# Setting up a Metaformer block: weights transposed four blocks to a bank, rows of ones written by DMA, temperatures loaded first

## What is computed

```
def attention(x, temperature, qkv_w, qkv_b, proj_w, proj_b):      # x after a layernorm over the channels
    qkv = x_flat @ qkv_w.T + qkv_b                  # per image 1024 tokens x 576
    q, k = l2norm(q), l2norm(k)                     # 8 heads of 24
    attn = softmax(einsum('bhnd,bhmd->bhnm', q, k) * temperature)
    return einsum('bhnm,bhmd->bhnd', attn, v) @ proj_w.T + proj_b

x = x + attention(ln(x), ...)
t = tokens(x)
# gate: softmax over 4 experts, the best 2 of each token, weights renormalised
h = gelu(einsum('bsd,edh->ebsh', ln(t), w1) + b1)
t = t + sum_e masked[e] * (einsum('ebsh,ehd->ebsd', h, w2) + b2)
```

## Time and profile before

| | |
|---|---|
| median of 3 runs | 2733.79 us |
| the runs | 2739.15, 2733.28, 2733.79 us |
| the profiled execution's own time | 2741.01 us |
| its span, first to last instruction | 2739.1 us |
| mean granted clock of TensorE | 0.971 |
| PE, DVE, ACT, POOL busy | 90%, 61%, 65%, 52% of the span |
| of it the setup | up to 38.66 us, where the next block's first transpose starts |

### The profile page before, as it was taken

The page is one execution under the profiler, slowest core; times in us unless marked ns, Lnnn a source line. Parts: engine busy times, 40 slices in busy tenths (PEclk is TensorE's granted clock), DMA queues, the critical chain, the costliest instruction groups (busy, mean ns, idle before and its releaser), DMA issues. The chain is left out here.

```text
span 2739.1 us, 58873 instructions
## 1 busy us (share of the span) xinstructions
PE 2465.8 (90%) x18693; PEld 1295.9 (47%) x18693; DVE 1683.5 (61%) x4886; ACT 1780.7 (65%) x2228; POOL 1420.5 (52%) x1137
## 2 busy tenths in 40 slices
PE   3699999999989999989999973999999999999975
PEld 2333333333333333333333321777777777777754
DVE  6557766866766766676676655555555555555522
ACT  2487777777778777767777852555565556555542
POOL 2334435534543543543454323677777777777750
PEclk9799999999999999999999987999999999999987
DMA  4221112112112111211211243444444444444429
GB/s 91 58 51 41 50 49 58 48 42 54 51 44 60 48 49 47 58 41 45 59 48 45 77 162 128 179 155 155 177 155 162 169 155 170 160 158 174 153 79 332
DMA packets 160322, 276.49 MB, mean 101 GB/s; under 512 B 21568, under 2 KB 129584, under 8 KB 150624
## 3 DMA queue, kind: packets, MB, share of 16 engines
q1 hardware_dynamic: 141648, 245.37, 27.8%
q0 software_dynamic: 13392, 27.97, 2.8%
q10 hardware_dynamic: 5056, 0.42, 0.3%
HBM read 174.07 MB, written 49.69 MB: 82 GB/s over the span
## 5 line engine op out<-in xcount | busy, mean ns | idle before, releaser
L788 ACT ACTIVATE probs<-ps_s 128x1024 f32<-128x1024 f32 x1024 | 1011.9, 1023 | 282.6 <-PE ps_s L687 260.0
L1360 POOL TENSOR_TENSOR h_split<-h_f,h_split 128x512 f16<-128x512 f32 x444 | 550.7, 1241 | 238.3 <-ACT h_f L1337 231.0
L1333 ACT ACTIVATE h_split<-ps_h,packs 128x512 f16<-128x512 f32 x444 | 305.2, 687 | 391.1 <-PE ps_h L1287 368.8
L1287 PE MATMUL ps_h<-m_xn_t,packs 128*128 128x512 f16 x2220 | 552.4, 380 | 0.5 <-DVE m_xn_t L1422 0.5
L700 PE MATMUL ps_o<-probs,v_aug 128*32 128x512 f32 x4096 | 550.6, 610 | 0.4 <-ACT probs L788 0.4
L1054 POOL TENSOR_TENSOR inv_norm<-sumsq,minus_half 128x16 f32<-128x16 f32 x128 | 378.0, 2953 | 312.4 <-DVE sumsq L997 307.6
L1301 PE MATMUL ps_y<-packs,h_split 128*128 128x192 f16 x5328 | 511.9, 245 | 0.9 <-POOL h_split L1360 0.9
L1301 PEld LDWEIGHTS ps_y<-packs,h_split 128*128 128x128 f16 x5328 | 453.0, 97 | 105.7 <-POOL h_split L1360 1.9
L687 PE MATMUL ps_s<-stacks_odd 98*128 98x512 f16 x1024 | 301.5, 386 | 17.0 <-DMA stacks_odd<-heads 10.2
L687 PE MATMUL ps_s<-even 98*128 98x512 f16 x1024 | 299.0, 383 | 11.6 <-ACT probs L788 5.7
L1337 ACT ACTIVATE h_f<-ps_h,packs 128x512 f32<-128x512 f32 x444 | 302.0, 680 | 0.0
(11 more groups left out here) (213 smaller groups left out, 2812.6 us busy)
## 6 DMA issues: line engine op xcount, KB each, us to landing
packs<-expert_pack SPq DMA_DIRECT2D x74, 1635.0 KB, 6.6
even<-heads SPq DMA_DIRECT2D x192, 96.0 KB, 2.4
stacks_odd<-heads SPq DMA_DIRECT2D x192, 96.0 KB, 2.4
tile_rows<-sorted_rows SPq DMA_DIRECT2D x37, 400.0 KB
tokens<-in_x_dram SPq DMA_DIRECT2D x17, 768.0 KB, 5.3
y_in<-y_tokens SPq DMA_DIRECT2D x16, 768.0 KB, 8.9
out_dram<-y_out SPq DMA_DIRECT2D x16, 768.0 KB, 7.1
even<-heads SPq DMA_DIRECT2D x128, 48.0 KB
```

The costliest lines, as they stand in the source:

```text
L788: act.activation(probs[:, u % PRING, :], ps_s[:, u % 2, :, :].rearrange("p f n -> p (f n)"), ACT.Exp).then_inc(s_probs, 1)
L1287: mm = pe.matmul(ps_h[:, n % HBUF, :], w1(par, slot, w, k), xn_t[0:rows_k, par, c, :], start=(i == 0), stop=(i == 4))
L1333: act.activation(h_split[:, n % HSPLIT, 0, :], ps_h[:, n % HBUF, :], ACT.Gelu, bias=bias1(par, slot, k), scale=1.0 / WSCALE)
L1360: pool.tensor_tensor(h_split[:, n % HSPLIT, 1, :], h_f32[:, n % HBUF, :], h_split[:, n % HSPLIT, 0, :], ALU.subtract).then_inc(s_h, 1)
```

## The change

Three edits, all in the setup.

- The temperatures are loaded by SP's first DMA instead of its eighth, on a semaphore of their own (`s_temps`). DVE waits for that one before the shift, and for the two biases at the end of the block.
- DVE's two memsets of the rows of ones are gone. SP issues two DMAs instead that copy a tile of ones (`ones16`, made by POOL) into both stacks, 2 partitions x 64 x 128 half precision values each, after its loads and before the stores into `sorted_rows`.
- PE transposes four blocks of 96 into one bank before it signals, so that there are six groups in place of 24 single blocks; DVE copies a group out with one instruction of 384 columns, or with two of 192 where a group spans the gap between the two weights.

```
@@ sync
+            sp.dma_start(temps[:, :], temp.rearrange("h a b -> (a b) h").to_broadcast([P, NH])).then_inc(s_temps, 16)
             for lo in (0, C):
                 sp.dma_start(w_src[:, 0:6, lo:lo + C], wv).then_inc(s_wload, 16)
                 sp.dma_start(w_src[:, 6:WJ, lo:lo + C], wp).then_inc(s_wload, 16)
...
-            sp.dma_start(temps[:, :], temp.rearrange("h a b -> (a b) h").to_broadcast([P, NH])).then_inc(s_bload, 16)
+
+            sp.wait_ge(s_const, 6)
+            for stack in stacks:
+                sp.dma_start(stack[KROWS:SROWS, 0, :, :].rearrange("r h n -> r (h n)").rearrange("r (a b) -> r a b", b=P),
+                             ones16[0:SROWS - KROWS, :].unsqueeze(1).to_broadcast([SROWS - KROWS, NH * NTOK // P, P])
+                             ).then_inc(s_ones, 16)
@@ tensor
             for s, lo in ((0, 0), (1, P), (2, 64)):
-                for j in range(WJ):
+                for j in range(0, WJ, 4):
                     if n >= 2:
                         pe.wait_ge(s_wt_free, n - 1)
-                    pe.transpose(ps_m[:, n % 2, 0:HC], w_src[:, j, lo:lo + P], ident[0:HC, 0:HC]).then_inc(s_wt, 1)
+                    for i in range(4):
+                        mm = pe.transpose(ps_m[:, n % 2, i * HC:(i + 1) * HC], w_src[:, j + i, lo:lo + P], ident[0:HC, 0:HC])
+                    mm.then_inc(s_wt, 1)
                     n += 1
@@ vector
-            for stack in stacks:
-                dve.memset(stack[KROWS:SROWS, 0, :, :], 1.0).then_inc(s_ones, 1)
-            dve.wait_ge(s_bload, 48)
+            dve.wait_ge(s_temps, 16)
...
-                for j in range(WJ):
+                for j in range(0, WJ, 4):
                     dve.wait_ge(s_wt, n + 1)
-                    at = j * HC + (NE if j * HC >= QKV else 0)
-                    dve.tensor_scalar(w_f32[:, s, at:at + HC], ps_m[:, n % 2, 0:HC], WSCALE, None,
-                                      ALU.mult).then_inc(s_wt_free, 1)
+                    lo, hi = j * HC, (j + 4) * HC
+                    if hi <= QKV:
+                        mm = dve.tensor_scalar(w_f32[:, s, lo:hi], ps_m[:, n % 2, 0:hi - lo], WSCALE, None, ALU.mult)
+                    else:
+
+                        dve.tensor_scalar(w_f32[:, s, lo:QKV], ps_m[:, n % 2, 0:QKV - lo], WSCALE, None, ALU.mult)
+                        mm = dve.tensor_scalar(w_f32[:, s, PROJ:PROJ + C], ps_m[:, n % 2, QKV - lo:hi - lo], WSCALE, None,
+                                               ALU.mult)
+                    mm.then_inc(s_wt_free, 1)
                     n += 1
...
+            dve.wait_ge(s_bload, 32)
@@ scores, first unit of an image
-            pe.wait_ge(s_ones, 4)
+            pe.wait_ge(s_ones, 2 + 2 * 16)
```

More of the change, by code:

```diff
@@ L433, in attention_phase @@
     s_bload = sem("s_bload")
+    s_temps = sem("s_temps")
     s_wt = sem("s_wt")
```

## The result

The changed kernel takes 2727.1 us (median of 15 runs, 2722.15 to 2729.02), the kernel before 2733.74 (15 runs, 2729.76 to 2739.15): 6.6 us less, ratio 0.9973 with a 95% interval of 0.9965 to 0.9981. That is inside the range and a little over half of the gain that I forecast.

A forecast was written before the change was run, and what follows sets the result against it. The last engine to arrive bounds the setup: ACT 25.3, DVE 24.4, POOL 25.3 us, end put at 25.7, first transpose at 26.4 instead of 38.66. The 12.3 us saved take the median from 2733.8 to 2721.5 us; range 2717 to 2729.

The forecast's parts named there:

- the prediction's own sign: Attention block's first transpose, L740: forecast near 26.4 us; a start at 30 us or later would show the prediction wrong.
- The shift, 7.2 us: Setup, DVE: temperatures loaded first land at 5.5 us, eleven instructions keep their 1.72 us, shift done at 7.2.
- PE and DVE, 24.4 us: Setup: PE starts at 9.6, six groups of transposes take 5.3 us until 14.9, DVE's untouched rest ends at 24.4.
- The margin of 1.3 us for `bias_g`: Setup, PE: the small loads for L528 land by 13.6 us, in time by 1.3 us before the transposes end.
- ACT, 25.3 us: Setup: ACT's 28 DMAs still take 18.1 us to issue after the shift at 7.2, unless the queue backs up.
- POOL, 25.3 us: Setup: stores into `sorted_rows` land at 23.4 us, delayed 1.0 by the ones and 3.0 by ACT's DMAs; POOL needs 1.90 more.
- The sum: Setup's end: latest of the arrivals put at 25.7 us, PE's first transpose at 26.4, 12.3 us less than before.
- the rival of the stores: Setup, POOL: delayed stores hold POOL back, at the far end first transpose at 35.3 us and 2730.4 us; 16%.
- The rival's half form: Setup, POOL: half of the stores' excess delay puts POOL's arrival at 30 us and the time at 2725.8 us.
- The two-queue rule of the Trainium skill: Setup's copies of ones: each runs on two engines, so the stores' shares on those two come later than all others.
- Kept to the end: After the setup: the whole earlier start carries through to the end; the rival that a later wait swallows it, 2733, 3%.
- The clock: TensorE in the first image: rival that its return to 2.4 GHz falls elsewhere, making it slower, 2741.5 us at 40 us; 3%.

The follow-up runs named there:

- e10: The changed kernel, nothing altered, measured and profiled a second time; 4.6 us less than the kernel before, ratio 0.9985.
- e3: The changed kernel with each copy of ones cut in two, one DMA per partition; 6.8 us less than the kernel before, ratio 0.9978.
- e8: e6 with each copy of ones cut in two, one DMA per partition, still ahead of the stores; ratio 0.9955 to the kernel before.
- e4: The changed kernel with POOL's two DMAs into y_tokens moved ahead of its wait for the stores; ratio 0.9960 to the kernel before.
- e5: The changed kernel with ACT's 28 bias DMAs issued by SP in the attention block instead; ratio 0.9962 to the kernel before.
- e7: e6 with SP's two copies of ones issued behind the six stores instead of ahead of them; ratio 0.9948 to the kernel before.
- e6: The changed kernel with the moves of e4 and e5 together; 14.9 us less than the kernel before, ratio 0.9942.
- e1: The kernel before with the grouped transposes alone, memsets and late temperatures kept; 0.4 us more than the kernel before, ratio 1.0002.
- e11: e7 with DVE casting and splitting all weight columns but the last four earlier; 11.5 us less than the kernel before, ratio 0.9957.
- e2: The changed kernel with the 24 single transposes and copies of before, no grouping; 8.9 us less than the kernel before, ratio 0.9973.
- e9: The changed kernel with the temperatures loaded last of the eight again; 2.7 us less than the kernel before, ratio 0.9986.

## Why the prediction came out as it did

The range held, the direction too, and the size was off: 2721.5 forecast, 2727.1 measured. The mechanism was half right. The last arrival does set the end of the setup, and an earlier end is kept; but the last engine was another than forecast, and by the prediction's own sign (L740 at 30 us or later) it was wrong: L740 starts at 30.93. That the median lies in the range is in part luck, since the forecast's own 2720 to 2724 misses it, and the ratio of the second measurement (e10) would put it at 2729.6, just outside. By its steps:

- *The shift, 7.2 us.* Measured 7.02, from two errors that cancel. The temperatures landed 3.2 us after issue, not 4.7; the eleven instructions took 2.9 us, not 1.72, because two of them stretched (below).
- *PE and DVE, 24.4 us.* Measured 23.58. The weights came at 9.36 (the row names POOL, whose constant PE also waits for, but that one was made by 2 us), and the 24 transposes took 4.75 us and not 5.3. The margin of 1.3 us for `bias_g` was not there: it landed at 4.79 + 9.1 = 13.9, and L537 started at 13.97. In e10, e3 and e8 PE waited 0.9, 1.5 and 1.3 us for it.
- *ACT, 25.3 us.* Measured 28.51. The 28 issues took 21.5 us and not 18.1; "unless the queue backs up" was the part that came true. Its drain adds 0.4.
- *POOL, 25.3 us.* This is the step that failed, in the term "POOL needs 1.90 us more". POOL ended at 30.6. 2.3 us of the difference are the stores, which landed at 25.7 and not 23.4. The other 3.0 are a drain that I had left out, though it stands in the trace of before, from 20.4 to 23.2. Moved ahead of the wait (e4), the two DMAs that it waits for cost nothing, and ACT was last.
- *The sum.* 30.6 and not 25.7 as the last arrival. The case that happened is the rival of the stores, in a milder form, with the drain on top; I gave it 16%. Both mechanisms named for it were shown: ACT's 28 DMAs cost 3.6 us (e5), for which I had taken 3.0, and the copies of ones 2.2 us (e7), for which I had taken 1.0. Together with the 0.5 us by which e7's last store is still later than before they are the 6.4 us from 19.37 to 25.74. The rival's half form (30 us, 2725.8) comes close by luck, since 3.0 of its excess are the drain and not the stores. Its argument that the queues were full until 19.4 us was a misreading too: the mean share of the 16 DMA engines was 1.0 until 18 us, 0.26 in the next microsecond and nothing after it.
- *The two-queue rule of the Trainium skill* ("DMA: Bandwidth & Descriptors", "Why a DMA increments its semaphore by 16 and not by 1"). By it a DMA of two partitions runs on two engines, and one of the cut copies, whose slowest dimension is the 64 rows, on 16. The traces agree that the cut copies are spread wider: of the copies' packets of 256 bytes never more than 4 were under way at once in the kernels with the two whole copies, and 12 and 13 in e3 and e8, where each is cut in two; for the stores' own packets it is 18 to 20. They don't bear out what I drew from it: the stores were late, but spreading the copies over more engines did not bring them back (22.4 us in e8, 22.1 in e6). Putting the copies behind the stores did (19.9 in e7). The cost is that the copies are ahead of the stores, and not how few engines they use; why 64 KB ahead of them cost 2.2 us stays open.
- *Kept to the end.* Yes, as far as these medians can tell: start and time agree within 2 us in e1 to e4, e6 to e10 and the changed kernel, and fall apart by 4.5 and 5.1 in e5 and e11.
- *The clock.* It came down earlier (0.50 from 54 to 58 us, where it was 1.00 before) and was at 0.50, the level of 1.2 GHz, when the first scores began, as before. PE is busy throughout in the last three windows below; the clock is at 0.70 in the second of them and back in the third. The stretch from the first to the second image's scores is 85.4 us (101.1 to 186.5) against 84.7 (108.5 to 193.2). Not the rival that I priced. Windows of the changed kernel, with the granted clock behind the five engines' busy times:

```profile
54.00:58.00 4.00, 2.03 (x13) 1.12 (x11) 2.98 (x10) 1.02 (x1) 1.99 (x1) 0.50 0.00 0
102.00:106.00 4.00, 4.00 (x15) 2.05 (x14) 1.46 (x5) 3.50 (x4) 0.00 (x0) 0.50 0.24 61
106.00:110.00 4.00, 4.00 (x21) 1.60 (x20) 1.57 (x6) 2.64 (x4) 0.00 (x0) 0.70 0.00 0
110.00:114.00 4.00, 4.00 (x29) 1.15 (x26) 2.70 (x14) 3.60 (x4) 0.00 (x0) 1.00 0.08 14
```

## What to carry to other kernels

When blocks end in a meeting of all engines, list every engine's arrival with its drain, and shorten the last one; e1 took 4.9 us off DVE's path and e2 gave 3.9 back, both without any effect. Work that is started earlier is also work that collides earlier: the 28 small DMAs were harmless behind the stores and cost 3.6 us among them. And profile the same kernel twice before a difference of 2 us between two profiles is given a cause. What isn't needed in a block, and what is waited for at its end only because it was issued there, belongs into another one.

## What the runs showed that I had not expected

- *POOL's drain.* It waits for the DMAs that POOL itself issued: 0.24 us with none under way (e4, e6, e7, e8, e11), 2.4 us with two of 96 KB and no DMAs of ACT (e5), 2.8 in the kernel before, where ACT's had only just begun, and 3.9, 5.0, 5.2, 5.5, 7.0 us beside ACT's (changed, e2, e9, e10, e3). ACT and SP, which had issued 36 and 16 DMAs in the changed kernel, drained in 0.4 us. ACT did not wait for its data: in e10 its drain ended at 28.2, and its last DMA, issued at 27.2, landed after 32, since none of its kind (L186) took less than 5.4 us. It does wait for its own instructions: in e5, where ACT issues nothing behind its two long writes, its drain takes 13.97 us, from 7.0 until the second write ends at 21.0.
- *Issuing stalls.* In the changed kernel SP's second copy of ones took 1.9 us to issue and one store up to 4.9, in place of 0.45, while ACT's 28 issues took 21.5 us for 18.1. The stall follows the position in the queue, not the DMA: in e7 it hit the second copy, at 6.0 us.
- *Two small DVE copies took eight times as long.* L555 and L556 took 1.41 and 1.35 us in place of 0.16 and ended with POOL's memset (4.05 to 5.48). In the kernel before POOL was idle then, and in e9, where they run at 14.15 beside an idle POOL, they take 0.16 and 0.17 us again. The Trainium skill ("SBUF — State Buffer", "Who interferes with whom") has copies and scalings of DVE in a fast mode blocked by a GpSimd instruction that holds the shared ports; the trace agrees, with 5.51 and 5.52 against 5.48 for the ends.
